# Two waits of TensorE set to later events in a graph network kernel: first products wait for the scan two groups back, relation products for the additions one group back

## What is computed

```python
def _edge_conv(x, src, dst, W1, b1, W2, b2, n_nodes):     # three times, relu between
    xi = x[dst]
    xj = x[src]
    m = jnp.concatenate([xi, xj - xi], axis=-1)
    h = jax.nn.relu(m @ W1 + b1) @ W2 + b2
    agg = jax.ops.segment_max(h, dst, num_segments=n_nodes)
    return jnp.where(jnp.isfinite(agg), agg, 0.0)
...
x = _layernorm(x + edge_network(x))
# relation layer
row = src + n * rel
inv = 1.0 / deg                                            # deg: edges of each row
msg = node_emb[dst] * inv[row][:, None]
agg = jax.ops.segment_sum(msg, row, num_segments=r * n)    # then (r, n, e)
out = jnp.einsum('rij,rnj->ni', weights, agg)
x = _layernorm(x + relu(out))
```

## Time and profile before

| | |
|---|---|
| median of 3 runs | 9480.66 us (9475.42 to 9495.2) |
| the profiled execution | 9484.52 us |
| its span, first to last instruction | 9482.7 us |
| PE matmuls busy | 6710.9 us (71%), 41098 instructions |
| PE weight loads busy | 5255.2 us (55%) |
| DVE busy | 5275.8 us (56%) |
| ACT busy | 4898.1 us (52%) |
| POOL busy | 6935.8 us (73%) |
| TensorE clock granted, mean | 0.909 of full speed |

### The profile page before, as it was taken

How to read it: one execution, slowest core, us unless ns; L and a number is a source line. 1 busy time by engine, 2 the same in 40 slices (tenths; PEclk the granted TensorE clock), 3 DMA queues, 4 the chain that set the end, 5 groups by cost and what they waited for, 6 DMA issues and landing times. The chain is left out here.

```text
span 9482.7 us, 160130 instructions
## 1 busy us (share of the span) xinstructions
PE 6710.9 (71%) x41098; PEld 5255.2 (55%) x41098; DVE 5275.8 (56%) x9611; ACT 4898.1 (52%) x11866; POOL 6935.8 (73%) x7196
## 2 busy tenths in 40 slices
PE   6777777876677777777667777777768555555555
PEld 5666666665565565666555666666654343333333
DVE  5666666665577666666546555555556333333334
ACT  2444444443344444444434444444446777777776
POOL 4777777776777777777777777777764777777775
PEclk9999999998899999999989999999999777777777
DMA  5665656664455555565545666656656222222222
GB/s 144 158 158 157 158 158 158 157 159 126 127 151 148 153 154 153 148 149 149 151 125 147 166 161 162 164 157 157 159 154 248 54 54 54 54 54 54 54 54 67
DMA packets 896156, 1259.78 MB, mean 133 GB/s; under 512 B 185847, under 2 KB 601079, under 8 KB 895270
## 3 DMA queue, kind: packets, MB, share of 16 engines
q1 hardware_dynamic: 650494, 784.23, 27.0%
q0 software_dynamic: 230048, 471.99, 22.6%
q10 hardware_dynamic: 15408, 0.88, 0.1%
HBM read 834.14 MB, written 424.01 MB: 133 GB/s over the span
## 5 line engine op out<-in xcount | busy, mean ns | idle before, releaser
L834 POOL DMA_INDIRECT agg<-tab_b,agg x5136 | 4984.5, 971 | 1596.2 <-issue 1527.3
L968 PE MATMUL ps<-tab_a 128*128 128x128 f32 x20544 | 3080.0, 284 | 3.4 <-issue 3.4
L968 PEld LDWEIGHTS ps<-tab_a 128*128 128x128 f32 x20544 | 2874.6, 202 | 4.1 <-issue 4.0
L966 PE MATMUL ps<-ident,agg 128*128 128x128 f32 x5136 | 1480.8, 288 | 1588.6 <-DMA agg<-tab_b,agg 1503.0
L1593 DVE TENSOR_TENSOR_SCAN agg<-agg,ps 128x512 f32<-128x512 bf16 x1284 | 1639.4, 1277 | 1689.8 <-PE ps L975 1687.7
L1279 ACT ACTIVATE agg<-ps 128x512 f32<-128x512 f32 x1284 | 766.8, 597 | 3475.2 <-PE ps L968 3442.3
L891 POOL DMA_INDIRECT work<-z_tab,work x1708 | 1611.6, 944 | 576.0 <-issue 501.3
L1163 PE MATMUL ps<-tab_a,work 128*128 128x256 f32 x3416 | 1228.0, 522 | 914.7 <-DMA work<-z_tab,work 611.6
L966 PEld LDWEIGHTS ps<-ident,agg 128*128 128x128 f32 x5136 | 753.1, 147 | 1824.6 <-issue 1420.3
L1270 ACT ACTIVATE tab_a<-tab_a 128x256 f32 x5136 | 1713.7, 404 | 52.6 <-issue 41.5
L1163 PEld LDWEIGHTS ps<-tab_a,work 128*128 128x128 f32 x3416 | 841.5, 258 | 1301.3 <-DVE tab_a L2038 1108.2
(11 more groups left out here) (252 smaller groups left out, 2982.0 us busy)
## 6 DMA issues: line engine op xcount, KB each, us to landing
agg<-row_two SPq DMA_DIRECT2D x1284, 256.0 KB
scan_rows<-agg SPq DMA_DIRECT2D x1284, 256.0 KB
agg<-tab_b,agg POOLq DMA_INDIRECT x5136
z_tab<-tab_a SPq DMA_DIRECT2D x84, 512.0 KB, 3.7
work<-z_tab,work POOLq DMA_INDIRECT x1708, 2.5
tab_b<-work SPq DMA_DIRECT2D x42, 448.0 KB, 3.1
work<-in_x SPq DMA_DIRECT2D x26, 448.0 KB, 5.6
z_tab<-work SPq DMA_DIRECT2D x14, 512.0 KB, 3.9
```

The costliest lines, as they stand in the source:

```text
L834: g.indirect_dma_start(rows[k][:, t, :], None, tab_b, bass.IndirectOffsetOnAxis(ap=idx[at.h][:, at.j * GT + t:at.j * GT + t + 1], axis=0)) ...
L966: mm(to, rows[at.k][:, t, :], ident[:, :], is_transpose=True, start=True, stop=False)
L968: last = mm(to, tabs[at.s][:, t, h * P:(h + 1) * P], hot_t[at.s][:, h, t * P:(t + 1) * P], start=False, stop=(h == 1))
```

## The change

Two waits of PE are set. In a layer's step, the first products of group G get a new wait, for the scan of group G-2. In the relation stage, the existing wait of the products of group g for the additions of group g-4 becomes a wait for the additions of group g-1. Nothing else is changed.

```diff
@@ step of PE in a layer
                 if live(0):
                     at = Lt(l, i, k)
+                    pe.wait_ge(s_scan, at.G + 1)
                     pe.wait_ge(s_hot, at.G + 1)
                     pe.wait_ge(s_tabs, at.G + 1)
                     pe.wait_ge(s_h1, at.G + 1)
@@ sum_tiles
                     g = i * LR + k
                     pe.wait_ge(s_got[k % LG], 64 * (2 * i + k // LG + 1))
                     pe.wait_ge(s_hr, g + 3)
-                    pe.wait_ge(s_acc, GT * g + 1)
+                    pe.wait_ge(s_acc, GT * g + 3 * GT + 1)
                     for t in range(GT):
```

## The result

The changed kernel takes 10239.03 us (median of 4 runs, 10212.94 to 10263.26) against 9482.06 us for the kernel before (4 runs): a ratio of 1.0796, 95% interval 1.0766 to 1.0826, or +757 us. The forecast was 10160 us, range 9950 to 10430. The profiled execution took 10263.26 us, the slowest of its four.

The account below looks back on a forecast made before the run. The prediction took POOL, at 4.99 us a group, to bound the kernel everywhere. Its terms 269 + 120 + 8 + 285 = +682 us on the profiled 9484.5 us gave 10166, forecast as 10160 us, range 9950 to 10430.

Parts of the forecast that it names:

- POOL's 4.99 us as the measure of everything: All stages: POOL's gathers set the pace, about 4.99 us a group; only a loop longer than that costs time.
- The loop of layer 0: Layer 0: first products, second products, end products, end masks and scan close a loop of mean 5.62 us, +269 us.
- The falls of the clock in layer 0: Layer 0: long PE gaps in every fourth group lower the clock, 75 falls of 107 at 1.6 us, +120 us.
- Layers 1 and 2: First products there: without end masks the loop is 4.68 us, under POOL's 4.99; +8 us, range -20 to +80.
- the cover of 0.3 us a group: Layer 2: margin by which the 4.68 us loop stays under POOL's pace; more in layer 1.
- The relation loop: Relation stage: products and additions alternate, 6.29 us at the lower clock, 4.50 at full; taken at 5.66, +285 us.
- the mixture: Relation stage: products' place between 1.99 us (full clock) and 3.78 us (lower), 0.48 before, taken as 0.65 after.
- What queues behind: Work behind both waits moves by the same delay, with slack; POOL will show waits for PE instead of "issue".
- nothing happens: Rival, whole kernel: POOL's pace covers both waits, about 9480 us; chance 0.05.
- Only one loop binds: Rival: at full clock the relation loop of 4.50 us hides under 4.99, leaving 9880 us; chance 0.08.
- The clock stays low: Rival: relation stage at 6.29 us a group and a fall at every long layer 0 gap, 10487 us; chance 0.12.
- Faster: Rival, layers 1 and 2: DVE's sort work meets fewer gathers, up to 145 us back, 9340 us; chance 0.03.

Follow-up runs that it names:

- e3: Changed kernel with both waits one group looser (scan of G-3, additions of g-2): 9489.73 us, ratio 0.9999 to the kernel before.
- e4: Changed kernel with DVE's order in layer 0 turned round, scan of G-2 before the end masks of G: 9840.18 us, ratio 1.0375.
- e9: Changed kernel plus 12 identity transposes per relation group before its waits, on an ordinary chip: 9901.9 us, ratio 1.0424.
- e12: Changed kernel plus 8 identity transposes in every fourth group of layer 0, order of the first products' waits kept: 10128.34 us, ratio 1.0664.
- e1: Kernel before plus only the first products' wait for the scan, relation wait as before: 9900.34 us, ratio 1.0428.
- e2: Kernel before with only the relation products' tighter wait for the additions: 9810.48 us, ratio 1.0326.
- e10: Changed kernel plus 8 identity transposes in every fourth layer 0 group, scan wait moved behind the other waits, ordinary chip: 10142.28 us, ratio 1.0664.
- e7: Kernel before plus 12 identity transposes per relation group, on the chip where the kernel before took 13132.98 us: 13229.48 us, ratio 1.0065.

## Why the prediction was right

- *POOL's 4.99 us as the measure of everything* held. Every stage whose loop was below it kept its time (layers 1 and 2, e3, e4's layer 0, e9's relation stage), every stage above it took its loop's length. That stretched gathers beside DVE's sort work make layer 1's 5.24 us fits the trace of before (they make 111 us, the stage is 107 us over 4.99 a group); in layer 2 they make only about 25 of 40 us.
- *The loop of layer 0*: put at 5.62 us a group at full clock, +269 us; e12 shows 5.61 us, (5.607 - 4.990) x 427 = +263 us. e4 showed that its parts were named rightly.
- *The falls of the clock in layer 0*: mechanism right, number off. I took 75 falls at 1.6 us, +120 us. It was 107 at 1.4 us, +153 us. The 75 were a choice between bounds, and the length of the gap would not have given the number: in layer 0 of the kernel before, of 14 gaps of 1.9 to 2.6 us with full clock ahead of them 5 had a fall behind and 9 had none. Why every long gap of the changed kernel has one stays open.
- *Layers 1 and 2*: put at +8 us, came at -8 us, within what these stages vary by. Their granted clock went up from 0.96 to 0.98 rather than down, and the cover of 0.3 us a group held. What is lost is as said, too: the fastest groups of these layers followed each other at about 3.5 us before and at 4.65 to 4.68 us now, the loop of 4.68 us.
- *The relation loop*: 6.29 us at the lower clock was measured at 6.28, and the clock decided, as said; e9 shows the other end. The mis-sized term is the mixture. I took 0.65 of the way from 1.99 to 3.78 us; PE's idle time before a group is now 1084.9 / 427 = 2.54 us, so products last 5.88 - 2.54 = 3.34 us, 0.75 of the way. That is +376 us instead of +285. It is the largest of the four misses: +91 us here, +33 for the falls, -6 for the loop of layer 0, -16 for layers 1 and 2, together 102 of the 103 us between the forecast +682 and the measured +785. I had no row that would fix it: the trace of before shows the clock only under the old gaps.
- *What was computed and what was chosen*: the loops came from rows and were met within 0.01 us. The number of falls and the mixture were chosen between bounds; they are 405 of the 682 us and came out 124 us short. That the total is as near as 0.8% owes something to luck.
- *What queues behind*: POOL's waits for PE appeared before L891 (406.8 us, 18.9 before), but not before L834, where that sign was wrong. There most of the idle time is still "issue" (1538.6 of 1993.9 us), only 22.3 us are put down to PE (37.2 before), and what grew is the wait for ACT's copy of the index list (L1262; 433.0 us against 31.7), as in the row at 1510.18. That copy stands in ACT's queue behind a relu that waits for PE, so POOL is held by PE through ACT.
- *The rivals*: "nothing happens" fell, and with it the advice of the Trainium skill, Perfetto Trace Analysis, section "Identifying the Most-Contended Engine", taken alone. By busy time POOL leads only before the change (73% against PE's 71%, after it 67% against 68%). The same section of the Trainium skill judges TensorE by its share of peak work and its weight loads instead of its matmul time, and by the weight loads POOL leads both times (73% against 55%, 67% against 53%). Neither measure shows a loop, and the kernel got 8% slower. "Only one loop binds" fell with e1 and e2. "The clock stays low" came true in layer 0, where every long gap brought a fall, and three quarters of the way in the relation stage. "Faster" had no ground: the gathers of layer 1 kept their pace, 5.23 against 5.24 us a group.

## What to carry to other kernels

A wait costs nothing or much, by the length of the loop that it closes: add up what runs from the waiting instruction once around back to it, divide by the number of groups that the loop spans, and compare with the pace of the engine that bounds the stage. With one group more room the loop spans two groups, so it counts half; in e3 nothing of the loss was left. Where the sum lies close to the pace, TensorE's clock decides, because the wait itself makes idle gaps, and the clock fell behind each of the long ones in layer 0; so work out the loop at both levels. And look for work in the queue between the awaited event and its predecessor that need not be there: turning two steps of DVE round (e4) gave layer 0 back as much as loosening the wait (5.00 and 4.99 us a group).

## What the runs showed of the hardware that I had not expected

- Work added to TensorE made a stage faster: 12 transposes a group, 1.47 us of PE's time, took the relation stage from 5.88 to 5.00 us a group by keeping the granted clock at 0.99 instead of 0.63.
- In layer 0 of the changed kernel the clock fell once per fourth group, 107 times in 107, with a gap of PE of 2.0 to 2.4 us each time; with the plain groups' gaps of about 1.5 us (1.52 in the timeline of e12) it never did. With the long gap shortened to 1.46 us there was no fall at all, nor with e10's plain gaps of about 1.7 us.
- The length of the gap alone does not decide. In the three layers of the kernel before, of the gaps with full clock ahead of them, none of 253 between 1.4 and 1.9 us had a fall behind it, 46 of 117 between 1.9 and 2.6 us had one, and 58 of 78 longer ones.
- The order of several waits before one instruction matters when the last to come is not at its place: with the scan's wait behind the others, the product started 0.22 to 0.23 us after the scan, with it ahead of them 0.05 us. An estimate from this: in all 1281 groups of the layers it would be 0.17 x 1281 = 218 us, where the loop binds.
- The relation stage's time in one and the same kernel spreads with the granted clock: e2 took 9779.56 us at 0.887 and 9863.81 us at 0.871, while the 13 runs of the kernel before on that chip, covered by POOL, stay within 0.3%.
- One chip ran the kernel before in 13133 us instead of about 9490 us. In e7 on that chip ACT and DVE stood still together for up to 9 to 10 us in the stretch shown, while PE issued a matmul of 0.37 us every 2.1 us. Only the comparison with the kernel before on the same chip showed that the kernels were not to blame.
